# Splitting the keys of an attention mixer into separate high and low buffers, with the tokens in two halves of the rows

## Time and profile before

| what | value |
|---|---|
| median of 3 runs | 3177.16 us (3176.27 to 3178.38) |
| the profiled execution | 3183.26 us, span 3181.4 us |
| PE busy | 2600.3 us (82%), 13374 matmuls |
| DVE busy | 2267.2 us (71%) |
| ACT busy | 1366.3 us (43%) |
| POOL busy | 943.2 us (30%) |
| first ysum (L364) of the mixer, last one | 50.27 us, 923.00 us |

### The profile page before, as it was taken

One profiled execution on the slowest core, in us unless ns is written; L12 is line 12 of the kernel. 1 busy time (PEld: TensorE's weight loads), 2 busy tenths in 40 slices (PEclk: granted clock), 3 DMA queues, 4 the chain that ended last, 5 costly groups with the idle time before them and its releaser, 6 DMA issues. The chain is left out here.

```text
span 3181.4 us, 47434 instructions
## 1 busy us (share of the span) xinstructions
PE 2600.3 (82%) x13374; PEld 1907.6 (60%) x13375; DVE 2267.2 (71%) x5978; ACT 1366.3 (43%) x2304; POOL 943.2 (30%) x943
## 2 busy tenths in 40 slices
PE   7999999999997999986666499983687785656776
PEld 3555555555556888875555399983476674334444
DVE  5777777777756989876555344436687776999997
ACT  1333333333332333334333256554565561655555
POOL 2001001000000000005666344448776640333333
PEclk9999999999998999995555699996787796666555
DMA  1000000000000000004222577762111100000000
GB/s 57 1 0 26 0 0 26 0 0 1 0 0 7 0 0 0 1 0 145 80 79 81 165 248 255 257 216 56 47 43 39 42 21 19 18 22 17 22 22 22
DMA packets 67222, 161.79 MB, mean 51 GB/s; under 512 B 12974, under 2 KB 30562, under 8 KB 66402
## 3 DMA queue, kind: packets, MB, share of 16 engines
q1 hardware_dynamic: 37578, 94.18, 9.1%
q0 software_dynamic: 21504, 44.99, 5.0%
q10 hardware_dynamic: 8064, 21.68, 2.2%
HBM read 63.89 MB, written 63.88 MB: 40 GB/s over the span
## 5 line engine op out<-in xcount | busy, mean ns | idle before, releaser
L353 DVE TENSOR_REDUCE pmax<-ppre 112x1 f32<-112x448 f32 x784 | 478.4, 624 | 128.3 <-PE ppre L211 126.3
L173 ACT ACTIVATE prob<-pscore 128x896 f32<-128x896 f32 x336 | 305.4, 917 | 589.4 <-PE pscore L243 492.1
L255 PE MATMUL pout<-prob,xkey 128*64 128x448 f32 x1344 | 326.9, 565 | 0.2 <-ACT prob L173 0.2
L211 PE MATMUL ppre<-xhl,yh 113*112 113x448 f32 x784 | 317.2, 406 | 6.5 <-DVE pmax L353 5.1
L211 PEld LDWEIGHTS ppre<-xhl,yh 113*112 113x112 f32 x784 | 138.3, 177 | 213.9 <-DVE pmax L353 153.0
L1622 POOL DMA_INDIRECT yg<-rows_out,place x224 | 230.6, 1029 | 62.4 <-issue 62.1
L242 PE MATMUL pscore<-yh,xhl 113*128 113x448 f32 x644 | 242.3, 376 | 0.0
L1042 POOL DMA_INDIRECT rows_in<-xn,idx x224 | 217.9, 973 | 66.0 <-issue 62.7
L243 PE MATMUL pscore<-yl,xhl 113*128 113x448 f32 x644 | 235.4, 366 | 0.0
L2078 POOL TENSOR_TENSOR yg<-y,gout 112x512 f32<-112x512 f32 x112 | 142.2, 1270 | 230.1 <-DVE y L2311 225.8
L1480 POOL TENSOR_TENSOR zl<-z,zh 128x448 fp32r<-128x448 f32 x126 | 144.7, 1148 | 214.0 <-ACT zh L1453 204.5
(11 more groups left out here) (372 smaller groups left out, 6645.5 us busy)
## 6 DMA issues: line engine op xcount, KB each, us to landing
wd<-down SPq DMA_DIRECT2D x63, 512.0 KB, 3.0
xb<-rows_in SPq DMA_DIRECT2D x63, 448.0 KB, 3.6
rows_out<-yb ACTq DMA_DIRECT2D x63, 336.0 KB, 3.2
out<-ho SPq DMA_DIRECT2D x28, 336.0 KB, 2.8
rows_in<-zero SPq DMA_DIRECT2D x15, 448.0 KB, 4.9
x<-in_xT SPq DMA_DIRECT2D x8, 600.2 KB
rows_in<-xn,idx POOLq DMA_INDIRECT x224, 2.6
yg<-rows_out,place POOLq DMA_INDIRECT x224
```

Of the source, the lines that this page charges most:

```text
L173: nc.scalar.activation(prob[j % 3][:, :, :], pscore[j % 2][:, :, 0:CH], ACT.Exp).then_inc(exped, 1)
L211: pe.matmul(ppre[k % 2][:, 0:CH], yh1[:, q * T:(q + 1) * T], xhl[b % 2][:, kc * CH:(kc + 1) * CH], start=True, stop=True).then_inc(pre_mm, 1)
L255: mm = pe.matmul(pout[i * LO:(i + 1) * LO, 0:CH], xkey[b % 2][:, 2 * j + i, :], prob[j % 3][:, i, :], start=(j == 0), stop=(i == 1 and j = ...
L353: nc.vector.reduce_max(pmax[:, q, kc:kc + 1], ppre[k % 2][:, 0:CH], AX.X).then_inc(pre_max, 1)
```

The core of the diff:

```diff
+KEYS_A = 1600
+KEYS_B = TOK - KEYS_A
+HALF = 1664
+PRE = 8
...
-                q, kc = k // CPI, k % CPI
-                pe.wait_ge(pre_max, g * TPC * CPI + k - 1) if k >= 2 else pe.wait_ge(pre_max, g * TPC * CPI)
-                pe.matmul(ppre[k % 2][:, 0:CH], yh1[:, q * T:(q + 1) * T],
-                          xhl[b % 2][:, kc * CH:(kc + 1) * CH], start=True, stop=True).then_inc(pre_mm, 1)
+                q, half, block = k // PRE, k % 2, k % PRE // 2
+                width = (KEYS_A, KEYS_B)[half] // (PRE // 2)
+                rows = slice(half * LO, half * LO + X1)
+                pe.wait_ge(pre_max, g * TPC * PRE + k - 1) if k >= 2 else pe.wait_ge(pre_max, g * TPC * PRE)
+                pe.matmul(ppre[half][:, 0:width], yh1[rows, q * T:(q + 1) * T],
+                          xh[b % 2][rows, block * width:(block + 1) * width], start=True, stop=True,
+                          tile_position=(half * LO, 0)).then_inc(pre_mm, 1)
...
-                for i in range(2 if j < SLOTS - 1 else 1):
-                    k = 2 * j + i
-                    out, keys = pscore[j % 2][:, i, 0:CH], xhl[b % 2][:, k * 128:(k + 1) * 128]
-                    pe.matmul(out, keys, yh[:], start=True, stop=False)
-                    mm = pe.matmul(out, keys, yl[:], start=False, stop=True)
-                    if j == SLOTS - 1 or i == 1:
-                        mm.then_inc(scores, 1)
-                    between()
+                keys = slice(j * 128, (j + 1) * 128)
+                for n, (x, y) in enumerate(((xh, yh), (xl, yh), (xh, yl))):
+                    if j == 0 and n == 0:
+                        pe.wait_ge(y_shifted, 2 * g + 1)
+                    if j == 0 and n == 2:
+                        pe.wait_ge(y_shifted, 2 * g + 2)
+                    for i in (1 - half, half) if j < SLOTS - 1 else (0,):
+                        rows = slice(i * LO, i * LO + X1)
+                        mm = pe.matmul(pscore[j % 2][:, i, 0:CH], x[b % 2][rows, keys], y[rows], start=(n == 0),
+                                       stop=(n == 2), tile_position=(i * LO, 0))
+                    if n < 2:
+                        half = between(half)
+                mm.then_inc(scores, 1)
+                return half
...
-                    if j == 1 and nxt is not None:
+                    if j == 0 and nxt is not None:
                         pe.wait_ge(y_out, 2 * (g + 2) - 1)
-                    run = first_pass if 1 <= j < SHIFT_SLOT else lambda: None
+                    run = first_pass if j < SHIFT_SLOT else lambda half: half
                     slot_pv(g, b, j)
-                    run()
+                    half = run(half)
+                if after is not None:
+                    if after[0] != b and nxt[0] == b:
+                        pe.wait_ge(xq_in, 16 * (after[0] + 1))
+                    pe.wait_ge(dvec, g + 2)
+                    make_y(g + 2, *after)
...
-                    take_y(g + 1)
-                    for k in range(TPC * CPI):
-                        if not first and k in (5, 11):
+                    for k in range(TPC * PRE):
+                        if not first and k in (9, 15):
...
                     shift_y(g + 1)
+                    if enter:
+                        take_y(g + 2)
```

More of the change, by code:

```diff
@@ L98, in mixer_phase @@
         w_in = sem("w_in")
-        x_in = [sem(f"x_in{i}") for i in range(2)]
+        x_in = sem("x_in")
+        key_in = [sem(f"key_in{i}") for i in range(2)]
+        xq_in = sem("xq_in")
         zeroed = sem("zeroed")
@@ L219, in shift, with slot_scores @@
                 mm.then_inc(shift_mm, 1)
[L221 removed]
+            def slot_scores(g, b, j, half, between=lambda half: half):
                 if j >= 2:
@@ L269, in project, with chunk, first_pass @@
                 mm.then_inc(proj_mm, 1)
[L271 to L280, removed]
+            def chunk(g, b, nxt, after, first=False):
+                todo = list(range(TPC * PRE)) if nxt is not None else []
+                def first_pass(half):
+                    if not todo:
+                        return half
+                    k = todo.pop(0)
+                    first_scores(g + 1, nxt[0], k)
+                    return k % 2
+                half = slot_scores(g, b, 0, 1)
                 for j in range(SLOTS):
-                    if j == 1 and nxt is not None:
+                    if j == 0 and nxt is not None:
                         pe.wait_ge(y_out, 2 * (g + 2) - 1)
-                    run = first_pass if 1 <= j < SHIFT_SLOT else lambda: None
[L285 to L289, removed]
                         if nxt[0] != b:
                             pe.wait_ge(x_split, 2 * (nxt[0] + 1))
-                        make_y(g + 1, *nxt)
+                            pe.wait_ge(key_in[nxt[0] % 2], 16 * (nxt[0] // 2 + 1))
+                    run = first_pass if j < SHIFT_SLOT else lambda half: half
+                    if j < SLOTS - 1:
+                        half = slot_scores(g, b, j + 1, half, run)
                     if j in PROJECT_SLOTS and not first:
@@ L388, in take_stats, with chunk @@
                     nc.vector.bn_stats(bns[:, g * TPC + q, :], h[:, g * TPC + q, :]).then_inc(stat_out, 1)
[L390 removed]
+            def chunk(g, first=False, last=False, enter=True):
                 if not last:
[L393 to L397 removed]
+                    for k in range(TPC * PRE):
+                        if not first and k in (9, 15):
+                            take_projected(g - 1, (9, 15).index(k))
+                        if not first and k == 18:
                             dve.wait_ge(proj_out, 4 * g)
                         take_max(g + 1, k)
[L400 removed]
+                        if not first and k == 18:
                             take_stats(g - 1)
                     shift_y(g + 1)
+                    if enter:
+                        take_y(g + 2)
                 else:
@@ L410, in _ @@
             take_y(0)
-            for k in range(TPC * CPI):
+            for k in range(TPC * PRE):
                 take_max(0, k)
             shift_y(0, first=True)
+            take_y(1)
             chunk(0, first=True)
-            with dve.Fori(1, NC - 1) as g:
+            with dve.Fori(1, NC - 2) as g:
                 chunk(g)
+            chunk(NC - 2, enter=False)
             chunk(NC - 1, last=True)
```

96 lines of the change are left out of this document (49 added, 47 removed).

## The result

The changed kernel has a median of 3228.43 us (3219.20 to 3236.45, 4 runs) against 3177.36 us before: ratio 1.016, interval 1.012 to 1.020. The change makes the kernel **slower by 51 us**. The forecast was 3239, +62. The 4 runs of the changed kernel lie in two pairs, 3236 and 3220. The profiled execution took 3236.45 us, 53.2 more than that of before.

A forecast was written before the change was run, and what follows sets the result against it. The loop through the first-pass buffer was taken to bound the changed kernel: +2.6 us a chunk times 27 is +70, less 6 and 2 once, +62, giving a median of 3239 us, range 3165 to 3345.

The forecast's parts named there:

- The loop Fc, maximum, Fb: First-pass buffer in a mixer slot: Fb waits for Fc's maximum, starting 1.11 us after Fc; slot 2.59 for 2.50.
- Fc: The first-pass product behind PV in a slot; its maximum was to start 0.39 us after it and take 0.57.
- Fb: Later first-pass product of a slot, sharing Fc's buffer; TensorE was to be there at 0.60 us and stand 0.5.
- Pairs at 0.20: Neighbouring products in different row groups of the mixer run side by side, a pair costing 0.20 us, not 0.40.
- Switches: Changes of tiling mode in the mixer, between row tiles and full array at projections: +0.20 us each, bounds 0 and 0.4.
- PV 10 to PV 11: Late slots of a chunk: 1.85 us before, +0.4 from slot 12's three scores in one row group and the shift's switch.
- The boundary: From PV 11 to PV 0 of the next chunk: 4.23 us before, load of PV 0 at 4.5 after, +0.3.
- VectorE's extras: Projections and statistics on VectorE push the next Fc or Fb back, together 0.5 us a chunk, 0.25 already included before.
- PV 0 to PV 10: The ten slots with first-pass products, extras included: 26.22 us before, 28.1 after, +1.9 a chunk.
- The clock: Rival: stalls in each mixer slot lower TensorE's clock; slot about 4 us, time above 3500; chance 0.04.
- Prologue and last chunk: Once per kernel: first query product at 18.61 instead of 25.14, -6.5 us; prologue maxima +0.8; last chunk -1.6.
- The faster rival: Matrix work bounds the mixer, maxima free buffers in time: slot 2.1 us, chunk 29.7, kernel 3099; chance 0.12.

The follow-up runs named there:

- blocks_apart: Changed kernel with a slot's score products ordered block by block, three of one row group, then three of the other: 3293.0 us against 3178.9 before the change.
- third_pair_first: Changed kernel with the second first-pass product behind the third pair of score products, not ahead of it: 3178.59 us against 3178.87 before the change, ratio 1.0003.
- half_reduce: Changed kernel with maxima over half of each product's columns and exp scaled by 1/16: 3163.9 us against 3178.9 before the change.
- three_third_early: three_and_third_pair with VectorE taking the projections ahead of maxima 8 and 14, not 9 and 15: 3114.38 us against 3213.5 before the change, ratio 0.969.
- three_buffers: Changed kernel with three first-pass buffers in turn, the bank of pmisc added to the two: 3244.1 us against 3209.0 before the change, ratio 1.0113.
- three_repeat: three_buffers with the first pair of score products of every slot done twice: 3244.56 us against 3213.5 before the change, ratio 1.009.
- three_and_third_pair: three_buffers with the second first-pass product behind the third pair of score products: 3182.56 us against 3209.0 before the change, ratio 0.9913.

## Why the prediction was right, point by point

- **The bound.** The loop Fc, maximum, Fb was named as the thing that no busy share shows. It came as forecast: Fb's load 1.08 after Fc's (511.01 to 512.09), 1.11 forecast from data to data; the load's wait 0.57, forecast 0.5; the slot 2.59, forecast 2.59. The maximum's 0.566 was 0.561.
- **Pairs at 0.20.** Right, shown by blocks_apart, and by the slot of 2.04 us without a wait, where the sum with 0.20 a pair gave 2.1. The PV record of two column tiles was a sound guide to row tiles.
- **Switches.** PV to PV with a projection took 3.38 (510.11 to 513.49), 0.79 more than a plain slot; 0.65 + 0.20 forecast. PV 10 to PV 11 took 2.24 (500.79 to 503.03), forecast 2.25. The boundary:

```profile
503.03 0.97 PE L260 MATMUL pout<-prob,xkey 128*64 128x448 f32 x4
...
504.68 0.63 PE L212 MATMUL pmisc<-xq,A 49*113 49x448 f32 x1
...
504.69 0.47 PE L246 MATMUL pscore<-yh,xh 49*128 49x448 f32 x1
...
505.72 0.62 DVE L362 CAST yh<-pmisc 113x448 fp32r<-113x448 f32 x1 [0.69 <-PE pmisc L212]
...
506.33 0.92 ACT L181 ACTIVATE prob<-pscore 128x896 f32<-128x896 f32 x1 [3.19 <-PE pscore L246]
...
506.79 0.61 DVE L391 COPY oT<-pout 128x448 f32<-128x448 f32 x1
...
507.50 0.92 ACT L181 ACTIVATE prob<-pscore 128x896 f32<-128x896 f32 x1 [0.25 <-PE pscore L246]
```

  PV 11 at 503.03 to PV 0 at 507.52 is 4.49, forecast 4.5. The new query product and slot 0's scores run partly together (0.63 is the first half of it only), yet VectorE's three copies and the exp set the time as forecast.
- **VectorE's extras: the term that was wrong.** I had 0.5 us for projections and statistics pushing the loop, and 28.1 for PV 0 to PV 10. It is 34.07 - 2.24 - 4.49 = 27.3. The slot that holds the first projection's take is 2.56 long (513.49 to 516.05), no longer than a plain one, and so are those at the statistics (2.60 and 2.62): VectorE's idle 0.9 in a slot takes it. The term was not wrong in kind: with the third pair ahead of the wait it shows (third_pair_first). Together the interval was 34.07 for 34.9, 21 us less over the mixer.
- **The clock: a rival that came in at the start only.** It had 4 chances in 100 and was priced for the whole mixer. What happened, in the execution with a trace, is that TensorE stays at the low level from the prologue through the first chunk; that costs 17 us. That idle time in the prologue and in the slots' waits keeps it there is argued, not shown. It was not in the sum. In that execution it offsets most of the 21 us above, so +62 for +53 is partly luck; the two faster runs are only 42 to 44 us above the kernel before, and the median of 51 mixes the two kinds.
- **Prologue and last chunk.** The first query product started at 16.93, not 18.61: probably because xq no longer shares its way with the next image's loads, which now start at 14.40, behind the split. Last chunk as forecast.
- **The skill on evacuation.** The kernel before emptied its two buffers just in time, the changed one stands 0.57 us a slot for them (512.09). The Trainium skill, "TensorEngine Tiling (Array Packing)", section "PSUM Bottleneck", warns that tiling speeds up TensorE but not the reading of its results. The runs agree, with one refinement: VectorE was not full (68%), it was the round trip that was too long, and half_reduce and three_third_early mend it in two ways.
- **The faster rival** (matrix work the bound) was priced with a chunk of 29.7. It needed a third buffer and an earlier take of the projections; then the chunk was 29.17.

## What to carry to other kernels

Where one engine feeds another through two buffers, compare the round trip of a buffer (product, latency, reduction, release, next load) with the work that the producer does between two uses; a change that halves that work gains nothing if the round trip was just covered by it, and it loses what is queued in order behind the wait. Place the work that needs no buffer ahead of the product that waits, then add a buffer, and give every user of a shared buffer an early taker. Read the granted clock of each variant before judging it: three_buffers lost it, and three_repeat, with more work, kept it.

## What the runs showed of the hardware

- The granted clock of TensorE can go up and down in a kernel whose PE is nearly always busy: three_buffers has PE records for 29.56 of 32.40 us in an interval at full clock, and falls in others; the changed kernel has 94% and keeps 1.00 once it is there (its four runs have mean clocks of 0.828 to 0.831 over the whole kernel). The Trainium skill, "TensorE: Matmul & The Clock Gate", section "A second HAM failure mode: psum-queue depth-cycling", describes such swings where TensorE is briefly idle again and again as it goes round its result banks; three_buffers shows them, three_and_third_pair, with nearly the same waits behind the projections, does not. What exactly tips it stays open.
- Two products of the row groups 0 to 63 and 64 to 127 that leave a wait together start within 0.01 us of each other, weight loads included (511.01 and 512.09 in the changed kernel); a plain fp32 product over 49 rows (L212) also shares the array with products of the other row group (504.68 to 505.31, with scores from 504.69; the records don't name the rows, that these are the other row group is inferred from the program).
- The time of a maximum is linear in its columns down to 192: 624 ns for 448, 561 mean for 400 and 384, 358 mean for 200 and 192, about 1.04 ns a column and 155 fixed.
